# The last attention layer of a four-layer kernel in eight half-batch stages per sequence, with the softmax sums added down to two key tiles by GpSimd and VectorE

## What is computed

```python
for e in range(4):                                   # expert e owns tokens 256e .. 256e+255
    xn = layernorm(x[:, e*256:(e+1)*256], w, b)      # own norm inside the layer
    m = 256 // 2**e                                  # and sees only its first m features
    q, k, v = xn[..., :m] @ q_w[:, :m].T + q_b, ...  # 8 heads of 32
attn = softmax(q @ k.T * 256**-0.5)                  # over all 1024 keys, no mask
o = attn @ v
out[e] = o[.., :m] @ o_w[:m, :m].T + o_b[:m] + x     # the first m features only; then x + out, layernorm
```

## Time and profile before

| | |
|---|---|
| median of 3 runs | 2882.44 us (2877.03 to 2883.87) |
| the profiled execution | 2881.5 us, its span 2879.5 us |
| the last layer | from 2000.5 us (its first DMA) to the end of the span |
| one sequence of it in the steady part | 98.8 us |
| in 99 us of it, busy | PE 87, DVE 64, ACT 35, POOL 22 |

### The profile page before, as it was taken

One profiled execution on the slowest core, in us unless ns is written; L12 is line 12 of the kernel. 1 busy time (PEld: TensorE's weight loads), 2 busy tenths in 40 slices (PEclk: granted clock), 3 DMA queues, 4 the chain that ended last, 5 costly groups with the idle time before them and its releaser, 6 DMA issues. The chain is left out here.

```text
span 2879.5 us, 44749 instructions
## 1 busy us (share of the span) xinstructions
PE 2316.8 (80%) x18544; PEld 1434.7 (50%) x18544; DVE 1519.7 (53%) x2671; ACT 894.6 (31%) x1265; POOL 600.6 (21%) x340
## 2 busy tenths in 40 slices
PE   3899999999999976574756488895498898888996
PEld 1455554555555546463645265554355555555553
DVE  2455545555555543555454264556556756665562
ACT  0233333333333334242423122220043233333332
POOL 3221112221112101101010133432102113212212
PEclk7899999999999998887978799998699999999998
DMA  6456655555654416565656211102442254235220
GB/s 145 89 108 114 119 111 106 108 111 114 117 117 89 97 33 242 197 236 200 234 193 243 83 44 44 59 30 65 141 126 87 82 146 141 75 98 156 81 77 30
DMA packets 235288, 337.57 MB, mean 117 GB/s; under 512 B 14816, under 2 KB 172880, under 8 KB 234832
## 3 DMA queue, kind: packets, MB, share of 16 engines
q1 hardware_dynamic: 232272, 334.07, 43.6%
q10 hardware_dynamic: 2816, 0.65, 0.1%
HBM read 206.10 MB, written 127.93 MB: 116 GB/s over the span
## 5 line engine op out<-in xcount | busy, mean ns | idle before, releaser
L1619 ACT ACTIVATE l1f_probs<-l1f_slot 128x1024 f32<-128x1024 f32 x240 | 241.3, 1022 | 427.9 <-PE l1f_slot L1792 294.7
L500 DVE TENSOR_REDUCE l0a_rowmax<-l0a_slot 128x4 f32<-128x1024 f32 (+1 forms) x256 | 293.3, 1156 | 124.4 <-PE l0a_slot L605 121.5
L443 ACT ACTIVATE l0a_probs<-l0a_slot 128x1024 f32<-128x1024 f32 (+1 forms) x256 | 248.7, 972 | 337.3 <-PE l0a_slot L605 322.1
L1682 DVE TENSOR_REDUCE l1f_rowmax<-l1f_slot 128x1 f32<-128x1024 f32 x240 | 287.5, 1218 | 102.0 <-PE l1f_slot L1778 101.6
L1792 PE MATMUL l1f_slot<-l1f_Qs,l1f_Ks 128*128 128x256 f32 x960 | 185.6, 321 | 40.6 <-DVE l1f_rowmax L1682 16.3
L1778 PE MATMUL l1f_slot<-l1f_Ks,l1f_Qs 96*128 96x512 f32 x480 | 172.6, 454 | 33.7 <-DMA l1f_Qs<-kq_rows 18.3
L1792 PEld LDWEIGHTS l1f_slot<-l1f_Qs,l1f_Ks 128*128 128x128 f32 x960 | 143.3, 203 | 111.0 <-DVE l1f_rowmax L1682 30.4
L600 PE MATMUL l0a_slot<-l0a_mask,l0a_ident 128*128 128x512 bf16 (+1 forms) x512 | 150.3, 376 | 25.5 <-issue 23.2
L600 PE MATMUL l0a_slot<-l0a_maskT,l0a_ident 128*128 128x512 bf16 (+1 forms) x512 | 148.8, 373 | 24.0 <-ACT l0a_probs L443 20.3
L1737 PE MATMUL l1f_os<-l1f_probs,l1f_V 128*32 128x256 f32 x1920 | 164.4, 394 | 2.1 <-ACT l1f_probs L1619 1.2
L545 PE MATMUL l0a_O<-l0a_probs,l0a_V 128*32 128x128 f32 x3840 | 156.1, 279 | 11.0 <-issue 11.0
(11 more groups left out here) (186 smaller groups left out, 4025.1 us busy)
## 6 DMA issues: line engine op xcount, KB each, us to landing
expert_outputs<-l0f_inter SPq DMA_DIRECT2D x64, 512.0 KB, 2.6
l0f_wide<-expert_outputs SPq DMA_DIRECT2D x32, 1024.0 KB, 10.0
l0a_Qs<-qk_rows SPq DMA_DIRECT2D x96, 256.0 KB, 7.8
l0a_Ks<-qk_rows SPq DMA_DIRECT2D x96, 256.0 KB, 14.9
l1f_Ks<-kq_rows SPq DMA_DIRECT2D x48, 512.0 KB, 6.9
l0f_f<-in_dram SPq DMA_DIRECT2D x10, 2048.0 KB, 15.7
qk_rows<-l0a_hi SPq DMA_DIRECT2D x32, 512.0 KB, 2.8
qk_rows<-l0a_lo SPq DMA_DIRECT2D x32, 512.0 KB, 4.2
```

Of the source, the lines that this page charges most:

```text
L443: exp_ready.by(act.activation(probs[:, t % 2, HG * g:HG * g + HG, 0:reach, :], s[:, :, 0:reach, :], ACT.Exp, scale=SCALE))
L500: max_ready.by(dve.reduce_max(rowmax[:, t, :, 2 * g:2 * g + 2], s[:, :, :, first:2 * P], AX))
L1619: exp_done.by(act.activation(probs[:, half, u - FIRST[i], :], s[:, :], ACT.Exp, scale=SCALE))
L1682: max_done.by(dve.reduce_max(rowmax[:, 2 * u + t:2 * u + t + 1], s[:, :], AX))
```

## The change

The four layers' functions are the same but for the last. (The clearing of semaphores at a layer's end is grouped in all of them.)

- **Stages.** A sequence is eight stages: stage 2b does the tr steps of the first key half of batch b, stage 2b+1 those of the second. In each run also the four pv steps of the half before, and the nat steps (four, or two) of a batch part three stages on. The front of the next sequence is spread over the stages by a table; the number ahead of a step is the offset of its sequence. Out and finish of a sequence run in stages 2 and 3 of the next body; "again" for the body's own sequence is in stage 5. `hi` and `lo` are one buffer each instead of two, so each projection waits for the bounce of the one before. SP's read-back ("stack") is a step of its own.
- **Sums.** For each unit, after the exponential of its second key half, POOL adds the two halves of the probabilities (`added`, 128x1024, two buffers), and DVE adds the two halves of that (`folded`, 128x512). The steps stand right behind the unit's tr step in the common list. The product with ones takes `folded` only, two key tiles instead of eight, in a **sum** step two stages later; DVE's reciprocal waits for that.
- **Bias.** POOL adds the output bias over each expert's width only (512, 256, 128 and 64 columns of `total` instead of 4 times 512).
- ACT's placing of the maxima is a step of its own, one stage after mT.

```diff
+    front = {0: [(1, "xT", 0), (1, "xT", 1), (1, "xT", 2), (1, "k", 0)],
+             1: [(2, "load", 0), (1, "q", 0)],
+             2: [(1, "stack k", 0), (1, "k", 1), (-1, "out", 0), (-1, "out", 1)],
+             3: [(1, "stack q", 0), (1, "q", 1), (-1, "finish", 0)],
+             4: [(1, "stack k", 1), (1, "v", 0), (1, "rest of q", 0)],
+             5: [(0, "again", 0), (1, "stack q", 1), (1, "v", 1), (2, "statistics", 0)],
+             6: [],
+             7: [(2, "normalise", 0)]}
+    for s in range(NSTAGE):
...
+        row = merged(nat[:len(nat) // 2], tr[:2]) + pv[:2] + merged(nat[len(nat) // 2:], tr[2:]) + pv[2:]
+        row = merged(row, front[s])
+        if half:
+            row = [step for at in row for step in ([at, (0, "add", FIRST[i] + at[2] - tr[0][2])] if at in tr else [at])]
+            row[2:2] = [(0, "sum", i - 1) if i else (-1, "sum", NB - 1)]
+            row[4:4] = [(placing[0], "place", placing[1])]
...
-        hi = sb("hi", [P, 2, T], f32r); lo = sb("lo", [P, 2, T], f32r)
+        hi = sb("hi", [P, T], f32r); lo = sb("lo", [P, T], f32r)
+        added = sb("added", [P, 2, HKT * QW])
+        folded = sb("folded", [P, 4, 2 * QW])
...
+                if kind == "again":
+                    pool.wait_ge(consts, 16 * NCONST)
+                    x_again.wait(pool, X)
+                    pool.tensor_tensor(total[:, :, :], total[:, :, :], total[:, :, :], ALU.add).then_inc(doubled, 1)
+                    pool.wait_ge(doubled, X + 1)
+                    for e in range(NE):
+                        part = total[:, 2 * e:2 * e + 2, 0:width[e]]
+                        x2_ready.by(pool.tensor_tensor(part, part, ob[:, 0:width[e]].unsqueeze(1).broadcast_to([P, 2, width[e]]), ALU.add))
+                if kind == "add":
+                    b = OF_UNIT[i]
+                    u = i - FIRST[b]
+                    exp_done.wait(pool, X, TR.index((i, 1)) + 1)
+                    fold_done.wait(pool, X, i - 1)
+                    add_done.by(pool.tensor_tensor(added[:, i % 2, :], probs[:, 0, u, :], probs[:, 1, u, :], ALU.add))
...
+                if kind == "add":
+                    b = OF_UNIT[i]
+                    add_done.wait(dve, X, i + 1)
+                    sum_done.wait(dve, X if b else X - 1, b if b else NB)
+                    fold_done.by(dve.tensor_tensor(folded[:, i - FIRST[b], :], added[:, i % 2, 0:2 * QW], added[:, i % 2, 2 * QW:], ALU.add))
+                if kind == "sum":
+                    norms(X, i)
...
+                    for u in range(units):
+                        h = BATCHES[b][u][0]
+                        last = mm(OS[b % 2][DH * u:DH * u + DH, 0, :], V[:, parity, kt, DH * h:DH * h + DH],
+                                  probs[:, half, u, QW * j:QW * j + QW], start=kt == 0, stop=kt == NT - 1,
+                                  skip_group_check=True, tile_position=(0, DH * u))
+                if kind == "sum":
+                    units = len(BATCHES[i])
+                    fold_done.wait(pe, X, FIRST[i] + units)
+                    for j in range(2):
+                        for u in range(units):
+                            last = mm(OS[i % 2][DH * u:DH * u + DH, 1, :], ones[:, :], folded[:, u, QW * j:QW * j + QW],
+                                      start=False, stop=j == 1, skip_group_check=True, tile_position=(0, DH * u))
+                    sum_done.by(last)
```

More of the change, by code:

```diff
@@ L1335, in tr @@
-    def tr(i):
-        return [("tr", FIRST[i] + u, half) for half in range(2) for u in range(len(BATCHES[i]))]
-    def pv(i, half):
-        return [("pv", i, NT // 2 * half + j) for j in range(NT // 2)]
-    def ahead(steps):
-        return [("ahead",) + s for s in steps]
-    def merged(*streams):
-        keyed = [((j + 0.5) / len(s), i, step) for i, s in enumerate(streams) for j, step in enumerate(s)]
-        return [step for _, _, step in sorted(keyed, key=lambda k: k[:2])]
-    front = [("xT", 0), ("xT", 1), ("xT", 2), ("load",), ("k", 0), ("q", 0), ("k", 1), ("q", 1), ("statistics",), ("v", 0), ("v", 1), ("rest of q",), ("normalise",)]
@@ L1359, in nested_width_attention_layer @@
-    steps += pv(3, 0)[2:] + ahead(nat(1)[2:4]) + pv(3, 1)[:2] + ahead(nat(1)[4:5]) + pv(3, 1)[2:] + ahead(nat(1)[5:])
-    steps += [("out", 0), ("out", 1)] + ahead([("mT", 1)])
-    steps += ahead(tr(0)[:1] + nat(2)[:1] + tr(0)[1:3]) + [("finish",)] + ahead(tr(0)[3:4] + nat(2)[1:2])
-    steps += ahead(merged(tr(0)[4:], nat(2)[2:5], front[12:])) + ahead(merged(nat(2)[5:], pv(0, 0)) + [("mT", 2)])
-    lead = [s[1:] for s in steps if s[0] == "ahead"]
-    unslotted = ("statistics", "normalise", "load", "again", "pv", "rest of q", "finish")
@@ new lines, in nested_width_attention_layer @@
+    steps = []
+    for s in range(NSTAGE):
+        i, half = divmod(s, 2)
+        n = len(BATCHES[i])
+        tr = [(0, "tr", 2 * FIRST[i] + n * half + u) for u in range(n)]
+        o, was = divmod(s - 1, NSTAGE)
+        pv = [(o, "pv", HKT * was + j) for j in range(HKT)]
+        o, part = divmod(s + 3, NSTAGE)
+        units = range(FIRST[part // 2], FIRST[part // 2] + len(BATCHES[part // 2]))[2 * (part % 2):2 * (part % 2) + 2]
+        nat = [(o, "nat", 2 * u + t) for u in units for t in range(2)]
+        row = merged(nat[:len(nat) // 2], tr[:2]) + pv[:2] + merged(nat[len(nat) // 2:], tr[2:]) + pv[2:]
[4 more added lines that the diff above has]
+            row[4:4] = [(placing[0], "place", placing[1])]
+        else:
+            row += [(o, "mT", part // 2)]
+            placing = o, part // 2
+        steps += row
@@ L1399, in nested_width_attention_layer @@
         own_ln = LayerNorm(sb, sem, "own", setup, 1)
-        slots = [ps(f"slot{i}", [P, 1024]) for i in range(NSLOT)]
+        schedule = Schedule(steps, slotted, [ps(f"slot{i}", [P, 1024]) for i in range(3)], NSEQ)
+        arrived = schedule.arrived
         OS = [ps(f"os{i}", [P, 2, QW]) for i in range(2)]
@@ L1459, in loop @@
-        def loop(eng, piece):
-            def body(b, last):
-                for n in range(2):
-                    for step in steps:
-                        if step[0] == "ahead":
-                            if not (last and n == 1):
-                                piece(step[1:], 2 * b + n + 1, 1 - n, not last, True)
-                        else:
-                            piece(step, 2 * b + n, n, True, None if last and n == 1 else False)
-            for step in lead:
-                piece(step, 0, 0, True, "alone")
-            for b in range(0, NSEQ // 2 - 1):
-                body(b, False)
-            body(NSEQ // 2 - 1, True)
@@ L1600, in piece @@
-                if kind == "mT":
-                    i = step[1]
-                    if is_ahead == "alone" and i == 0:
-                        act.wait_ge(cleared, 1); act.wait_ge(cleared_too, 2)
-                    maxT_ready.wait(act, B, i + 1)
-                    n = len(BATCHES[i])
+                    s = arrived(act, X, step)
+                    p = PROJECTIONS.index((kind, i))
+                    bounced[PROJECTIONS[p - 1]].wait(act, X - (p == 0))
+                    hi_ready.by(act.activation(hi[:, 0:used], s[:, 0:used], ACT.Identity,
+                                               bias=bias[:, i:i + 1]))
@@ L1671, in piece @@
-                    s = slots[at[("ahead",) + step] % NSLOT]
-                    lo_ready.by(dve.scalar_tensor_tensor(lo[:, j, 0:used], s[:, 0:used], bias[:, c:c + 1],
-                                                         hi[:, j, 0:used], ALU.add, ALU.subtract))
+                    p = PROJECTIONS.index((kind, i))
+                    bounced[PROJECTIONS[p - 1]].wait(dve, X - (p == 0))
+                    hi_ready.wait(dve, X, PROJECTIONS.index((kind, i)) + 1)
+                    s = schedule.slot(step)
```

433 lines of the change are left out of this document (191 added, 242 removed).

## The result

The changed kernel takes 3252.73 us in the median of 4 runs (3251.34 to 3255.7), against 2880.52 us (2877.03 to 2883.87, 4 runs) for the kernel before beside it. The ratio is 1.1289, with a 95% interval from 1.1274 to 1.1303. So it is slower by 372 us, and 3250 us had been forecast.

The account below looks back on a forecast made before the run. PE bounded the kernel before. Fold waits and POOL's stage 5 queue give a period of 135.2 + 7 + 6 = 148.2 us; 2092 + 115 + 889 + 119 + 31 = 3246, said as 3250 us, range 3110 to 3370.

Parts of the forecast that it names:

- the long value: A DVE fold waits for POOL's whole next addition, 0.69 + 2.36 us; the short value would save some 8 per sequence.
- The sum: Whole kernel: lead to 2092, first body 115, six bodies 889, last body 119, end 31, together 3246 us.
- The single buffers: In the lead, one `hi` and `lo` buffer makes the q projection wait for k's bounce, about 5 us.
- The walk of stages 1 to 4: Chain with blocked folds ahead of row maxima: stages 1 and 2 31.9 us, then 21.4 to the end of result statistics.
- Stage 5: POOL's addition 9 stands behind the load of "again": 30.9 us from statistics to its end, DVE waiting from about 16.
- The 7 us for DMA: Twelve read-backs between store and load in SP's queue delay the load by 0 to 11 us; 7 taken.
- Stages 6 and 7: Stage 6 with four nat and four tr steps reaches stage 7's first tr step at 52.3 us; stages 7 and 0 29.6.
- 6 for the clock: PE's lower clock after idling costs 0 to 15 us per sequence; 6 taken.
- PE busy some 80 of 148 us: Sign expected in the profile: PE's busy time per sequence, with a clock under 0.95.
- PE didn't stay the bound: Rival that PE stays the bound, fold waits covered: 10.8 us per sequence go, 2796 us; chance 0.08.
- Again is hidden: Rival: addition 9 doesn't stand behind the load, stages 5 and 6 some 30 us, period 119, 3065 us; chance 0.10.
- The clock stays low: Rival: PE at half clock most of the time, period some 175, 3410 us; chance 0.06.

Follow-up runs that it names:

- e1: The change with its stages but without additions, folds and sum step (ones take all eight key tiles again); 2867.07 us, 0.9953 of the kernel before.
- e2: The change with POOL's doubling and bias of `total` moved from stage 5 to stage 6; 3093.76 us, 1.0722 of the kernel before.
- e6: The change with POOL starting an addition only after the fold of the one before; 3195.04 us, 1.1076 of the kernel before.
- e9: e1 with POOL's additions and ACT's wait for them back, read by nothing, and doubling with bias in stage 6; 2897.43 us, 1.0046 of the kernel before.
- e12: e1 with two `hi` and `lo` buffers, as in the kernel before; 2869.11 us, 0.9949 of the kernel before.
- e3: The change with twelve read-backs moved from in front of the load of `total` to behind it; 3213.47 us, 1.1136 of the kernel before.
- e7: The change without folds (ones take four added key tiles), plus the edits of e2 and e3; 2922.68 us, 1.0132 of the kernel before.
- e8: The change with each fold one tr step later, plus the edits of e2 and e3; 3040.85 us, 1.0541 of the kernel before.
- e11: e10 with the next input's statistics moved from the end of stage 5 to stage 6; 2916.64 us, 1.0111 of the kernel before.
- e10: e7 without the edit of e3, so the loads in the change's order; 2916.95 us, 1.0111 of the kernel before.

## Why the prediction was right, and where it was off

The mechanism was right: folds held up and waiting in front of row maxima, and POOL's queue in stage 5, are what the loss consists of (e1, e2, e6). The time (3250 against 3252.73 us) and the period (148.2 against 147 to 150) agree; the steps behind them do so less evenly, and that the total agrees to 3 us is in part luck.

- **Fold beside addition.** I took the long value by the earlier trace rows. The held-up folds take 2.63 and 2.81 us, 0.69 and some 2 more, and e6 shows the cause: without an addition beside it every fold is at 0.69. The prediction had put "some 8 per sequence" on this; e6 measures some 7. (For e6 itself I expected less than my own step said.) The trace agrees with the rule of the Trainium skill that was cited (SBUF — State Buffer, Who interferes with whom). The same section of the Trainium skill counts `tensor_scalar` among the instructions that can take the shared pair, and e9's normalisation, 8.9 us for 2.7, agrees.
- **The sum.** The profiled execution of the change shows where its terms fall (the layer's first load, and the first tr step of the lead, of the second body and of the last):

```profile
2007.03 0.36 SPq L1441 DMA_DIRECT2D l1f_xn<-x  x1
...
2094.94 1.06 PE L1752 MATMUL l1f_slot<-l1f_Qs,l1f_Ks 128*128 128x256 f32 x4
...
2220.85 1.06 PE L1752 MATMUL l1f_slot<-l1f_Qs,l1f_Ks 128*128 128x256 f32 x4
...
3109.83 0.70 PE L1752 MATMUL l1f_slot<-l1f_Qs,l1f_Ks 128*128 128x256 f32 x4
```

  The first body took 125.9 us instead of 115. The six bodies took 889.0 us as forecast, the first five of them 149.5 in the mean and the sixth 141. The last body with its end took 144.1 us instead of 119 + 31 = 150. With the first tr step 2.9 us late the span is 8 us over the forecast 3246, and the profiled execution, 3255.7 us, lies 3 us above the median. The single buffers were put at 5 us: the lead, from its first load, took 87.91 us instead of 86.80, and e12 gives back 1. The 2092 us came near because the three earlier layers ended 6.5 us later in this execution.
- **The walk of stages 1 to 4.** From the end of the first tr step to the end of the result's statistics I had 31.9 + 21.4 = 53.3 us; the trace has 2536.16 to 2591.98, 55.8. The tr step behind the first held-up fold ends at 8.9 (forecast 8.7). The 2.5 us arise at the q projection, which ends at 14.1 instead of 11.7: it took 4.5 us instead of 1.86, the granted clock being 0.51 from 2543.8 to 2550.3; I had put the lower clock in stage 6 alone.
- **Stage 5.** From the statistics to the end of addition 9 I had 30.9 + 7 = 37.9; the trace has 2591.98 to 2630.95, 39.0. The 7 us for DMA were 8.3 (18.7 - 10.4). e3 takes them back by one edit of SP's order, but the period falls by only 4 to 7 us. DVE stood at fold 9 from 15.7 us on, where I had about 16.
- **Stages 6 and 7.** To the first tr step of stage 7 I had 52.3 + 7, and 6 for the clock; measured 61.6, so some 2 more than without the clock. Stages 7 and 0 took 30.3 (29.6). Over the whole sequence, 147.7 us, some 4 us are left above the walk and the DMA's 8.3, where 6 were put on the clock. Only the q projection shows them as the clock's; no run parts the rest.
- **What was wrong.** "PE busy some 80 of 148 us" came out as 90 to 94. I had counted the removed work at the full clock and let the clock act on the chain only.
- **The rivals.** PE didn't stay the bound. "Again is hidden" was priced at 3065 us; e2, which makes it true, gives 3094 us with a period of 126.3 instead of 119, since the hold-ups and a clock of 0.81 remain. "The clock stays low" fell: 0.75 to 0.78 on the mean is neither of its levels throughout.
- **After the fact I was too hopeful.** The expectations of e7 and e8 took the period down to PE's work. They left out the statistics and the held-up normalisation on DVE in front of row maxima, and that PE's steps behind such stalls are slow: 1.22 instead of 0.74 us behind the 4.7 us in e7, and behind the 3.9 us in the change. The hold-up of the normalisation is shown by e9, the stall behind the statistics by e7's trace and its move in e11. What keeps e10 at 102.5 to 107 us though PE has 4 us less work than in e9 is not settled: its trace has waits for Q, for row maxima and a clock of 0.89 to 0.93, and no run parts them.
